# One FFN product moved to a later half, with three reorderings on VectorE around it

## The chip, the cores and the metric

The kernel runs on one core of a Trainium2 chip. The metric is the device time of one execution in microseconds, median over the runs.

## The reference

Cut to what is computed. The input has 64 sequences of 128 tokens with 256 channels, the context 128 tokens with 192 channels.

```python
def xattn(x, context, ...):                      # 16 heads of 64
    q_in = x @ Wq + lora(x, q_down, q_up)
    org, ipa = context[:, :-4], context[:, -4:]   # 124 and 4 tokens
    k_in = org @ Wk + lora(org, ...); v_in = org @ Wv + lora(org, ...)
    out = attention(q_in, k_in, v_in) + attention(q_in, ipa @ Wk_ipa, ipa @ Wv_ipa)
    return out @ Wo + bo + lora(out, o_down, o_up)

def ffn(x, w1, conv_w, conv_b, w2):
    h = bit_linear(x, w1)                         # x rounded to 8 bits per token, w to -1, 0, 1
    h = silu(depthwise_conv1d(h, conv_w, conv_b)) # 3 taps along the tokens, 1024 channels
    return bit_linear(h, w2)

x = x + xattn(layernorm(x), context, ...)
x = x + ffn(layernorm(x), w1, conv_w, conv_b, w2)
```

## The kernel before

The 64 sequences are taken in 16 groups of 4. Each engine runs its own program, written out by hand in one order, and they meet only at semaphores. One iteration of `run_groups` is one group's attention, in 32 **halves** (n = 0 to 31). Two halves are a **chunk**: one sequence and four heads. Iterations 0, 1, 15 and the two of the drain are written out, 2 to 14 are a loop.

In iteration g, `steps(g, n)` does four things side by side: the attention of group g, what is left of the projections of group g (`project(g, n + 32)`), the projections of group g + 1 (`project(g.shift(1), n)`), the FFN of group g - 1 (`finish(g.shift(-1), n)`) and the rest of the FFN of group g - 2 (`finish(g.shift(-2), n + 32)`). Tables at the head of the file say at which half a step stands: names in N_ for the projections, in M_ for the FFN. A place above 31 falls into the next iteration.

**PE** does, at each even half, `p_v` (L477, probabilities times V, three chunks back), `transpose_p` (L486, two chunks back), `scores` (L499, this chunk) and `project_out` (L512, four chunks back), and then what the tables put into the half: Q (L442), K (L451) and V (L461) products at N_Q, N_K, N_V plus N_QUAD, the transposes of the normalised x (L431) at N_XT = 8. For the FFN: the transposes of the quantised x2 at M_QT = 13 (L575), eight tiles of the first product into one PSUM bank, psF (L590, halves 15, 16, 17, 19, 20, 21, 23, 24), each waiting for the eviction of the one before, and the second product (L611), in two parts of two sequences, at M_F2 = (36, 38), so halves 4 and 6 of the iteration two after the group's own. The second part waits for the eviction of the first (`fin_done`).

**VectorE (DVE)**, at each even half, in `attend`: sums and reciprocals of the previous chunk (L903, L905), then the maxima of this chunk (L908, L909, L911), which wait for the scores. ACT's exponentials (L750) wait for these, and the next scores on PE wait for the exponentials. POOL (L1226) scales the probabilities by the reciprocals, and PE's transposes wait for it. Behind `attend` DVE does, in this order, the rest of its FFN steps of group g - 2, its projection steps and its FFN steps of group g - 1: the V copy (L896) from PSUM in halves 14, 22, 29 and 5, statistics of the next x, variance (L848, L851) at half 3, normalisation (L855) at half 6, the low parts of the context (L886, L887) at 8 and of x (L891) at 9, x2 = x + attention (L1029) at 4 and 7, normalisation, maximum and quantisation of x2 in halves 9 and 10 (L855, L1040, L1046, L1049). A tile of the first product is evicted to a GB buffer (L1063) in its own half. The convolution's middle tap is ACT's (L776), the other two are DVE's: `conv_before` (L998) one half later, `conv_next` (L992) two, and `gate` (L1004) three. The second product is evicted (L1020) two halves after it, M_FIN.

**POOL** raises the variance of the next x to the power -1/2 at half 4 (L1209), and adds the output bias to the residual (L1264). **SP** issues the DMAs in order: CRAW and RRAW at 7, the output at FINISH_HALVES - 1 (half 8), the K rows of the short context at 10, V rows at 10, 18, 26 and 1, XRES at 12.

HP holds the hidden layer, eight rows of 512 a partition. XN2 (the normalised x2) and Q1 (its quantised form) lie in its rows 6, 7 and 5, the quantised hidden layer Q2 in the first half of every row. GBS are the four GB buffers.

Of the kernel before, what the change touches and what calls it, by code (L numbers as in the profile page):

```python
# [51 lines left out]
U_Q, U_K, U_V = (0, 3), (1, 4), (2, 5)  # L52


N_STATS, N_VAR, N_POW, N_NORM = 0, 3, 4, 6
N_XT = 8
N_CIN = 7
N_CSPLIT = 8
# [13 lines left out]
M_F1 = 15  # L72
# [3 lines left out]
M_HMAX = M_F1 + M_TILE[-1] + M_HOFF  # L76
M_HT, M_BC2 = M_HMAX + 2, M_HMAX + 4
M_Q2 = M_HMAX + 5
M_F2 = (M_HMAX + 8, M_HMAX + 10)
M_COPY = M_Q2 + 2  # L80
L_X2, L_NORM, L_QT, L_F2 = (4, 5), 7, 13, M_HMAX + 8
Q2_PLACE = (0, 0, 1, 1)
# [64 lines left out]
def program(nc, x, ctxT, cipaT, Wq, Wk, Wv, Wo, bo, q_downT, q_up, k_downT, k_up, v_downT, v_up, o_downT, o_up,  # L147
            alphas, Wk_ipa, Wv_ipa, w1T, conv_w, conv_b, w2T, out):
    with ExitStack() as ctx:
# [63 lines left out]
        HT = [HP[:, j // 2, :, j % 2] for j in range(CT)]  # L213
        h_flat = HP[:].rearrange("p k t i -> p (k t i)")
        h_rows = h_flat.rearrange("p (j t) -> p j t", j=CT)
        XN2 = h_rows[:, 6:8, :].rearrange("p a (b d) -> p (a b) d", d=DM)
        Q1 = h_rows[:, 5, :].bitcast(BF16).rearrange("p (b d) -> p b d", d=DM)
        Q2 = [h_rows[:, j, 0:T // 2].bitcast(BF16) for j in range(CT)]
        OUTT = h_rows[:, 0:NB, T // 2:T]
        HM = GB[1]  # L220
# [619 lines left out]
        def _(dve):  # L840
# [30 lines left out]
            def project(g, n):  # L871
                if n in (N_STATS, N_STATS + 1):
                    if n == N_STATS:
                        dve.wait_ge(x_in, g.count(16, 16))
                    for b in range(2 * (n - N_STATS), 2 * (n - N_STATS) + 2):
                        m = dve.bn_stats(BS[0][:, b, :], XIN[:, b, :])
                    if n == N_STATS + 1:
                        m.then_inc(ln1_stats, 1)
                if n == N_VAR:
                    variance(g, 0, ln1_stats, ln1_mv, ln1_var)  # L880
                if n == N_NORM:
                    dve.wait_ge(ln1_rstd, g.count(1, 1))
                    normalise(0, XIN, XIN).then_inc(ln1_done, 1)
                if n == N_CSPLIT:
                    dve.wait_ge(c_high, g.count(1, 1))
                    dve.tensor_tensor(CTH[1][:], CRAW[:], CTH[0][:].bitcast(F32), ALU.subtract)  # L886
                    dve.tensor_tensor(CTR[64:128, :], RRAW[64:128, :], CTR[64:128, :].bitcast(F32), ALU.subtract).then_inc(c_split, 1)  # L887
                if n == N_XT + 1:
                    for k in range(2):
                        dve.wait_ge(xt_high, g.count(2, k + 1))  # L890
                        dve.tensor_tensor(XT[1][:, k, :], psU[k], XT[0][:, k, :].bitcast(F32), ALU.subtract).then_inc(unit_free[k], 1)  # L891
                q = quad_at(n - N_V[0] - 1)
                if q is not None:
                    u = 2 + 6 * q + U_V[0]
                    dve.wait_ge(unit_full, g.count(UNITS, u + 1))
                    dve.tensor_copy(V[0:ORG, 0:2, 256 * q:256 * q + 256],  # L896
                                    psU[u % 2][0:ORG, :].rearrange("p (b n) -> p b n", b=2)).then_inc(unit_free[u % 2], 1)

            def attend(g, s):
                gc, c = chunk_at(g, s - 1)  # L900
                if gc.exists():
                    dve.wait_ge(exp_done, gc.count(CHUNKS, c + 1))
                    dve.tensor_reduce(SU[c % 2][:, 4:8], SM[c % 2][:, :, ORG:TOK], AX.X, ALU.add).then_inc(sum_done, 1)  # L903
                    dve.wait_ge(sum_done, gc.count(CHUNKS, c + 1))
                    dve.reciprocal(RC[c % 2][:], SU[c % 2][:]).then_inc(rec_done, 1)  # L905
                if g.exists():
                    dve.wait_ge(s_full, g.count(CHUNKS, s + 1))
                    dve.tensor_reduce(MX[s % 2][:, 4:8], psS[:, :, ORG:TOK], AX.X, ALU.max, negate=True).then_inc(max_done, 1)  # L908
                    dve.tensor_reduce(MX[s % 2][:, 0:4], psS[:, :, 0:ORG], AX.X, ALU.max, negate=True)  # L909
                    dve.wait_ge(max_done, g.count(CHUNKS, s + 1))  # L910
                    dve.tensor_tensor(SM[s % 2][:, :, ORG:TOK], psS[:, :, ORG:TOK],  # L911
                                      MX[s % 2][:, 4:8].unsqueeze(2).broadcast_to([P, 4, IPA]), ALU.add).then_inc(sub_done, 1)
# [97 lines left out]
            def finish(g, n):  # L1010
# [30 lines left out]
                if n == M_NORM + M_SCALE:  # L1041
# [5 lines left out]
                    m.then_inc(q1_scaled, 1)  # L1047
                    dve.wait_ge(q1_scaled, g.count(1, 1))
                    dve.tensor_scalar(Q1, XN2, MAGIC, None, ALU.subtract).then_inc(q1_done, 1)  # L1049
                j = tile_at(n - M_F1 - M_LAG[2])  # L1050
                if 0 <= j < CT:
                    conv_next(g, j)
                j = tile_at(n - M_F1 - M_LAG[1])
                if 0 <= j < CT:
                    conv_before(g, j)
                j = tile_at(n - M_F1)
                if 0 <= j < CT:
                    dve.wait_ge(f1_full, g.count(CT, j + 1))
# [2 lines left out]
                    if j >= 4:  # L1061
                        dve.wait_ge(h_done, g.count(CT, j - 3))
                    dve.tensor_tensor(GB[j % 4].rearrange("p b t -> p (b t)"), psF, BC[:], ALU.mult).then_inc(g_done, 1)  # L1063
                j = tile_at(n - M_F1 - M_LAG[4])
                if 0 <= j < CT:
                    gate(g, j)
# [55 lines left out]
            low_part(2)  # L1122
            low_part(4)
            for n in range(EARLY_HALVES, HALVES):
                project(At(0), n)
                if n == LORA_O + 1:
                    dve.wait_ge(w_in[2], 16)
# [42 lines left out]

            def steps(g, n):
                if n % 2 == 0:
                    attend(g, n // 2)
                if g.reg is None and g.off == 0:
                    ternary(n)
                if g.shift(-2).exists():
# [135 lines left out]
```

## Time and profile before

| what | value |
|---|---|
| median of 3 runs | 1551.39 us (1551.12 to 1552.87) |
| the profiled execution | 1551.65 us |
| its span, first to last instruction | 1549.7 us |
| mean granted TensorE clock | 0.983 |
| PE busy | 1423.8 us, 92% |
| DVE busy | 1211.9 us, 78% |
| ACT busy | 1178.9 us, 76% |
| POOL busy | 661.4 us, 43% |
| POOL's power of the next x (L1209) | 1.02 us each |
| DMA, mean | 30 GB/s |

The page gives per engine the busy time and, for groups of instructions, the mean duration, the idle time just before them and what ended it. Matmul rows overlap, since their ends are modelled; what a step costs PE is read from start to start. The timeline gives the start, the duration, engine, line, operation, tiles (output <- inputs) and count of instructions in order of time, and in brackets the idle time before a row with its releaser.

### The profile page before, as it was taken

Reading aid. Unit: us, or ns where it says so; the run is one execution under the profiler, and the core shown is the slowest. Engines: PE = TensorE matmul, PEld = TensorE weight load, DVE = VectorE, ACT = ScalarE, POOL = GpSimd, SP = SyncE. Lnnn points to the kernel's source line nnn. Section 1 sums busy time; section 2 is a strip of 40 time slices with the busy share of each in tenths; the row PEclk is TensorE's granted clock in tenths of the full one; section 3 lists DMA queues with packets and bytes.
Section 4 is the critical chain, followed back from the end, with each engine's and each line's share of the span. In section 5 each row is a group of like instructions: output and inputs, shape, how many; then the busy total and the mean of one; then the engine's idle time right before and its main releaser. Section 6 shows DMA issues by size and latency. Waiting matters only on the chain.

```text
span 1549.7 us, 33116 instructions
## 1 busy us (share of the span) xinstructions
PE 1423.8 (92%) x10650; PEld 1157.1 (75%) x10650; DVE 1211.9 (78%) x3059; ACT 1178.9 (76%) x3909; POOL 661.4 (43%) x1058
## 2 busy tenths in 40 slices
PE   7899999999999999999999999999999999999772
PEld 4688788787877778787877878787787877878541
DVE  4363698887969888786988878798787878788788
ACT  3477787978878797887879787787978778796842
POOL 2354454444435444443544444444444444444520
PEclk9999999999999999999999999999999999999985
DMA  9100001000000100000010100001010000100000
GB/s 280 48 30 16 31 16 45 1 28 30 28 29 14 43 0 31 27 28 29 14 43 1 36 21 28 29 14 43 1 41 16 28 29 14 43 1 27 3 15 14
DMA packets 41144, 47.13 MB, mean 30 GB/s; under 512 B 3024, under 2 KB 35216, under 8 KB 41104
## 3 DMA queue, kind: packets, MB, share of 16 engines
q1 hardware_dynamic: 41104, 46.62, 9.7%
q8 instruction: 22, 0.36, 0.1%
q14 instruction: 18, 0.15, 0.0%
HBM read 36.13 MB, written 10.49 MB: 30 GB/s over the span
## 4 chain that ended last, share of the span: by engine, by line
PE 51%; DVE 20%; ACT 20%; issue 8%; DMA 1%; DVEq 0%; ACTq 0%; SPq 0%; POOL 0%
PE PS L499 10%; ACT SM L750 8%; PE PS L461 8%; PE PS L512 5%; PE PS L442 5%; PE PS L477 5%; PE PS L486 5%; PE PS L451 4%; PE PS L611 3%; ACT HP L776 2%; PE PS L590 2%; DVE GBS L1081 2%; DVE GBS L1063 2%; ACT QM L718 2%; ACT GBS L781 2%
## 5 line engine op out<-in xcount | busy, mean ns | idle before, releaser
L1226 POOL TENSOR_TENSOR SM<-SM,RC 128x496 f32<-128x496 f32 (+1 forms) x512 | 332.1, 670 | 743.5 <-DVE RC L905 743.5
L750 ACT ACTIVATE SM<-PS,MX 128x124 f32<-128x124 f32 x1024 | 359.4, 366 | 150.5 <-DVE SM L911 148.4
L499 PE MATMUL PS<-KT,QM 128*128 128x128 f32 x2048 | 277.8, 279 | 29.8 <-ACT SM L750 29.7
L499 PEld LDWEIGHTS PS<-KT,QM 128*128 128x128 f32 x2048 | 249.1, 192 | 45.4 <-ACT SM L750 44.7
L750 ACT ACTIVATION_READ_ACCUMULATOR SM<-PS,MX 128x1 f32 x1024 | 212.0, 207 | 0.0
L1257 POOL TENSOR_TENSOR OTl<-OF,OTh 128x256 fp32r<-128x256 f32 x256 | 198.5, 775 | 12.2 <-ACT OF L744 12.2
L742 ACT ACTIVATE OTh<-PS 128x256 fp32r<-128x256 f32 x256 | 100.4, 392 | 109.8 <-PE PS L477 108.7
L486 PE MATMUL PS<-IDF,SM 128*128 128x128 f32 x1024 | 168.4, 287 | 11.5 <-POOL SM L1226 11.3
L909 DVE TENSOR_REDUCE MX<-PS 128x4 f32<-128x496 f32 x256 | 170.0, 664 | 0.2 <-issue 0.2
L477 PE MATMUL PS<-PT,V 128*64 128x128 f32 x2048 | 168.8, 286 | 0.1
L477 PEld LDWEIGHTS PS<-PT,V 128*64 128x64 f32 x2048 | 106.9, 136 | 82.0 <-issue 74.8
L736 ACT ACTIVATE PT<-PS 128x512 f32<-128x512 f32 x256 | 156.9, 613 | 0.4 <-PE PS L486 0.4
L486 PEld LDWEIGHTS PS<-IDF,SM 128*128 128x128 f32 x1024 | 107.8, 141 | 57.8 <-issue 37.7
L908 DVE TENSOR_REDUCE MX<-PS 128x4 f32<-128x16 f32 x256 | 41.2, 161 | 124.9 <-PE PS L499 124.8
L776 ACT ACTIVATE HP<-GBS,CB,CW 128x512 f32<-128x512 f32 x128 | 111.3, 870 | 26.1 <-DVE GBS L1063 16.1
L1004 DVE SCALAR_TENSOR_TENSOR HP<-GBS,HP 128x512 f32<-128x512 f32 x128 | 109.1, 853 | 23.0 <-ACT GBS L781 22.2
L1063 DVE TENSOR_TENSOR GBS<-PS,BC 128x512 f32<-128x512 f32 x120 | 82.0, 683 | 54.7 <-PE PS L590 53.3
L512 PE MATMUL PS<-WOh,OTh 128*128 128x256 f32 x512 | 123.3, 322 | 0.7 <-POOL OTl L1257 0.7
L992 DVE SCALAR_TENSOR_TENSOR HP<-GBS,CW,HP 128x508 f32<-128x508 f32 x128 | 119.3, 932 | 0.1
L998 DVE SCALAR_TENSOR_TENSOR HP<-GBS,CW,HP 128x508 f32<-128x508 f32 x128 | 103.6, 809 | 17.6 <-ACT HP L776 14.1
L442 PE MATMUL PS<-XTh,WQh 128*128 128x512 f32 x256 | 107.2, 419 | 0.0
L512 PE MATMUL PS<-WOl,OTh 128*128 128x256 f32 x512 | 102.4, 281 | 0.0
(166 smaller groups left out, 3512.9 us busy)
## 6 DMA issues: line engine op xcount, KB each, us to landing
XIN<-in_x SPq DMA_DIRECT2D x16, 512.0 KB, 3.5
XRES<-in_x SPq DMA_DIRECT2D x16, 512.0 KB, 3.5
out_y<-HP SPq DMA_DIRECT2D x15, 512.0 KB, 3.0
CRAW<-in_ctxT SPq DMA_DIRECT2D x16, 256.0 KB, 2.7
RRAW<-in_ctxT SPq DMA_DIRECT2D x32, 128.0 KB, 2.8
QM<-in_Wq SPq DMA_DIRECT2D x1, 1024.0 KB, 9.0
GBS<-in_Wo SPq DMA_DIRECT2D x1, 1024.0 KB, 13.7
k_ipa_columns<-HP SPq DMA_DIRECT2D x1, 1024.0 KB, 5.1
```

Source lines behind the costliest of these rows:

```text
L442: m = mm(bank, WQ[w][:, k, P * tile:P * tile + P], XT[xt][:, k, :], start=(i == 0), stop=(i == 5))
L461: m = mm(bank[:, 256 * b:256 * b + 256], c[:, tok], w[:, cols], start=(i == 0), stop=(i == 4))
L477: m = mm(psO[r:r + DH, h // 2, :], V[:, b, DH * (4 * q + h):DH * (4 * q + h) + DH], PT[:, h, :], start=True, stop=True)
L486: m = pe.transpose(psT[:, h, :], SM[c % 2][:, h, :], IDF[:])
L499: m = mm(psS[:, h, :], QM[:, 2 * q + h // 2, h % 2, TOK * b:TOK * b + TOK], KT[:, 2 * q + h // 2, b, :], start=True, stop=True)
L512: m = mm(psY[b // 2][:, b % 2, :], OT[ot][c % 2][:, a, :], WO[w][:, 2 * q + a, :], start=(q == 0 and i == 0 and b % 2 == 0), stop=(q == QU ...
L736: act.activation(PT[:], psT, ACT.Identity).then_inc(pt_done, 1)
L750: m = act.activation(SM[s % 2][:, h, 0:ORG], psS[:, h, 0:ORG], ACT.Exp, bias=MX[s % 2][:, h:h + 1], accum_out=SU[s % 2][:, h:h + 1])
L776: act.activation(HT[j].rearrange("p (b t) -> p b t", b=NB), GB[j % 4], ACT.Identity, bias=CB[:, j:j + 1], scale=CW[:, j, 1:2]).then_inc(t1 ...
L909: dve.tensor_reduce(MX[s % 2][:, 0:4], psS[:, :, 0:ORG], AX.X, ALU.max, negate=True)
L1226: m = pool.tensor_tensor(part, part, RC[c % 2][:, 4 * i:4 * i + 4].unsqueeze(2).broadcast_to(shape), ALU.mult)
L1257: pool.tensor_tensor(OT[1][c % 2][:], OF[:], OT[0][c % 2][:].bitcast(F32), ALU.subtract).then_inc(ot_done, 1)
```

## The change

It does five things.

- M_F2 goes from (36, 38) to (36, 41): PE does the second FFN product of the second two sequences in half 9, not 6. Its eviction on DVE goes from half 8 to 11, and FINISH_HALVES with it, so SP's output DMA goes from half 8 to 11.
- XN2 and Q1 move out of HP into the GB buffers 2, 3 and 1.
- On DVE the eviction of a first-product tile stands ahead of the two taps of its half, not behind.
- On DVE the V copy stands between the sums and the maxima of a half. That changes the order in halves 14 and 22, where it stood behind the maxima; at 5 and 29 there are none.
- N_VAR, N_POW, N_NORM go from 3, 4, 6 to 5, 6, 7.

```diff
-N_STATS, N_VAR, N_POW, N_NORM = 0, 3, 4, 6
+N_STATS, N_VAR, N_POW, N_NORM = 0, 5, 6, 7
...
-M_F2 = (M_HMAX + 8, M_HMAX + 10)
+M_F2 = (M_HMAX + 8, M_HMAX + 13)
...
-        XN2 = h_rows[:, 6:8, :].rearrange("p a (b d) -> p (a b) d", d=DM)
-        Q1 = h_rows[:, 5, :].bitcast(BF16).rearrange("p (b d) -> p b d", d=DM)
+        gb_flat = GBS[:].rearrange("p i b t -> p (i b t)")
+        XN2 = gb_flat[:, 2 * T:4 * T].rearrange("p (b d) -> p b d", d=DM)
+        Q1 = gb_flat[:, T:2 * T].bitcast(BF16).rearrange("p (b d) -> p b d", d=DM)
...
-                j = tile_at(n - M_F1 - M_LAG[2])
-                if 0 <= j < CT:
-                    conv_next(g, j)
-                j = tile_at(n - M_F1 - M_LAG[1])
-                if 0 <= j < CT:
-                    conv_before(g, j)
                 j = tile_at(n - M_F1)
                 if 0 <= j < CT:
                     dve.wait_ge(f1_full, g.count(CT, j + 1))
...
+                j = tile_at(n - M_F1 - M_LAG[2])
+                if 0 <= j < CT:
+                    conv_next(g, j)
+                j = tile_at(n - M_F1 - M_LAG[1])
+                if 0 <= j < CT:
+                    conv_before(g, j)
...
             def steps(g, n):
                 if n % 2 == 0:
-                    attend(g, n // 2)
+                    attend_sums(g, n // 2)
+                if g.exists():
+                    value_copy(g, n + HALVES)
+                if g.shift(1).exists(1):
+                    value_copy(g.shift(1), n)
+                if n % 2 == 0:
+                    attend_maxima(g, n // 2)
```

The rows below are from the loop's iteration. In them `x16` and `x2` are counts, `REGISTER_ALU` is the arithmetic of a wait, and the lines of the changed file are one to five higher.

On PE in halves 6 to 9, from half 6's output product; before:

```order
L512 MATMUL PS<-WOh,OTl 128x256 x2
L131 REGISTER_ALU
L451 MATMUL PS<-CTh,WKh 128x512
L451 MATMUL PS<-CTl,WKh 128x512
L451 MATMUL PS<-CTh,WKl 128x512
L451 MATMUL PS<-CTR,WKRh 128x512
L451 MATMUL PS<-CTR,WKRl 128x512
L607 REGISTER_ALU
L611 MATMUL PS<-W,HP 128x256 x16
L461 MATMUL PS<-WVh,CTh 128x256
```

And now, from half 8's output product:

```order
L513 MATMUL PS<-WOh,OTl 128x256 x2
L428 REGISTER_ALU
L131 REGISTER_ALU
L432 MATMUL PS<-IDF,XIN 128x128 x8
L608 REGISTER_ALU
L612 MATMUL PS<-W,HP 128x256 x16
L478 MATMUL PS<-PT,V 64x128 x4
L487 MATMUL PS<-IDF,SM 128x128 x4
```

The 16 matmuls of the second product stood between K and V and now stand behind the transposes of x, ahead of half 10's chunk.

On DVE from half 8 to the start of half 10, before:

```order
L911 TENSOR_TENSOR SM<-PS,MX 128x4x4
L1020 SCALAR_TENSOR_TENSOR HP<-PS,AD,HP 128x256 x2
L886 TENSOR_TENSOR CTl<-CRAW,CTh 128x512
L887 TENSOR_TENSOR CTR<-RRAW,CTR 64x512
L890 REGISTER_ALU
L891 TENSOR_TENSOR XTl<-PS,XTh 128x512
L890 REGISTER_ALU
L891 TENSOR_TENSOR XTl<-PS,XTh 128x512
L855 TENSOR_SCALAR HP<-X,MV,RS 128x256 x4
L1040 TENSOR_REDUCE AR<-HP 128x4
L903 TENSOR_REDUCE SU<-SM 128x4
```

And where the eviction stands now, at the end of half 10's steps and in half 11:

```order
L1051 TENSOR_SCALAR GBS<-GBS,AS 128x256 x4
L1054 TENSOR_SCALAR GBS<-GBS 128x1024
L1025 SCALAR_TENSOR_TENSOR HP<-PS,AD,HP 128x256 x2
L906 TENSOR_REDUCE SU<-SM 128x4
L908 RECIPROCAL RC<-SU 128x8
```

The eviction of the second product left its place ahead of the low parts and stands ahead of the sums of half 12.

On DVE in halves 20 to 22, from the maxima of half 20; before:

```order
L998 SCALAR_TENSOR_TENSOR HP<-GBS,CW,HP 128x4x127
L1058 REGISTER_ALU
L1063 TENSOR_TENSOR GBS<-PS,BC 128x512
L1004 SCALAR_TENSOR_TENSOR HP<-GBS,HP 128x512
L992 SCALAR_TENSOR_TENSOR HP<-GBS,CW,HP 128x4x127
L998 SCALAR_TENSOR_TENSOR HP<-GBS,CW,HP 128x4x127
L1058 REGISTER_ALU
L1063 TENSOR_TENSOR GBS<-PS,BC 128x512
L903 TENSOR_REDUCE SU<-SM 128x4
L905 RECIPROCAL RC<-SU 128x8
L907 REGISTER_ALU
L908 TENSOR_REDUCE MX<-PS 128x4
```

And now:

```order
L1057 REGISTER_ALU
L1062 TENSOR_TENSOR GBS<-PS,BC 128x512
L1003 SCALAR_TENSOR_TENSOR HP<-GBS,CW,HP 128x4x127
L1009 SCALAR_TENSOR_TENSOR HP<-GBS,HP 128x512
L1057 REGISTER_ALU
L1062 TENSOR_TENSOR GBS<-PS,BC 128x512
L997 SCALAR_TENSOR_TENSOR HP<-GBS,CW,HP 128x4x127
L1003 SCALAR_TENSOR_TENSOR HP<-GBS,CW,HP 128x4x127
L906 TENSOR_REDUCE SU<-SM 128x4
L908 RECIPROCAL RC<-SU 128x8
L898 REGISTER_ALU
L899 COPY V<-PS 124x2x256
```

Each eviction (L1062) stands ahead of its half's taps, and the V copy, which followed the maxima of half 22, stands ahead of them.

## Rows read from the trace of the kernel before

**Rows 1.** One loop period: us; PE, PEld, DVE, ACT, POOL busy; PEclk; DMA

```profile
701.80:791.95 90.15, 85.96 (x662) 70.67 (x661) 74.19 (x190) 72.47 (x244) 40.22 (x66) 1.00 0.08 25
```

**Rows 2.** Who PE waited for, whole run (us in total, times, longest)

```profile
PE PS L499 <- ACT SM L750: 29.7, 62, 1.1
...
PE PS L590 <- DVE GBS L1063: 17.8, 31, 2.5
```

**Rows 3.** Timeline of PE, halves 6 to 14 (start, us, line, tiles, count, idle)

```profile
701.80 1.92 PE L611 MATMUL PS<-W,HP 128*128 128x256 bf16 x16
703.47 0.36 PE L461 MATMUL PS<-WVh,CTh 128*128 128x256 f32 x1
...
704.82 0.66 PE L477 MATMUL PS<-PT,V 128*64 128x128 f32 x8
...
707.50 1.04 PE L431 MATMUL PS<-IDF,XIN 128*128 128x128 f32 x8
...
709.06 0.66 PE L486 MATMUL PS<-IDF,SM 128*128 128x128 f32 x4
710.66 1.16 PE L499 MATMUL PS<-KT,QM 128*128 128x128 f32 x8 [0.95 <-ACT SM L750]
...
715.67 0.66 PE L486 MATMUL PS<-IDF,SM 128*128 128x128 f32 x4
716.66 1.16 PE L499 MATMUL PS<-KT,QM 128*128 128x128 f32 x8 [0.34 <-ACT SM L750]
...
720.68 0.66 PE L486 MATMUL PS<-IDF,SM 128*128 128x128 f32 x4
721.17 1.06 PE L499 MATMUL PS<-KT,QM 128*128 128x128 f32 x8
```

**Rows 4.** Timeline of ACT, halves 8 to 12

```profile
708.14 1.09 ACT L711 ACTIVATE XTh<-PS 128x512 fp32r<-128x512 f32 x2
709.11 0.37 ACT L750 ACTIVATE SM<-PS,MX 128x124 f32<-128x124 f32 x1
...
715.12 0.36 ACT L750 ACTIVATE SM<-PS,MX 128x124 f32<-128x124 f32 x1 [3.37 <-DVE SM L911]
...
719.33 0.37 ACT L750 ACTIVATE SM<-PS,MX 128x124 f32<-128x124 f32 x1
```

**Rows 5.** Timeline of DVE, halves 8 to 12

```profile
707.00 0.17 DVE L908 TENSOR_REDUCE MX<-PS 128x4 f32<-128x16 f32 x1 [1.01 <-PE PS L499]
...
707.75 0.86 DVE L1020 SCALAR_TENSOR_TENSOR HP<-PS,AD,HP 128x256 f32<-128x256 f32 x2
708.53 0.94 DVE L886 TENSOR_TENSOR CTl<-CRAW,CTh 128x512 fp32r<-128x512 f32 x1
...
714.27 0.16 DVE L908 TENSOR_REDUCE MX<-PS 128x4 f32<-128x16 f32 x1
...
718.16 0.16 DVE L903 TENSOR_REDUCE SU<-SM 128x4 f32<-128x16 f32 x1
```

**Rows 6.** Timeline of DVE, halves 21 and 22

```profile
744.21 1.21 DVE L992 SCALAR_TENSOR_TENSOR HP<-GBS,CW,HP 128x508 f32<-128x508 f32 x1
745.34 0.73 DVE L998 SCALAR_TENSOR_TENSOR HP<-GBS,CW,HP 128x508 f32<-128x508 f32 x1
...
747.64 0.68 DVE L896 COPY V<-PS 124x512 f32<-124x512 f32 x1
```

**Rows 7.** Timeline of POOL, half 20

```profile
743.70 1.18 POOL L1264 TENSOR_TENSOR XRES<-XRES,BO 128x256 f32<-128x256 f32 x1
```

**Rows 8.** Timeline of PE, halves 23 and 28

```profile
748.37 0.51 PE L451 MATMUL PS<-CTh,WKh 128*128 128x512 f32 x1 [0.37 <-DVE V L896]
...
761.37 1.16 PE L499 MATMUL PS<-KT,QM 128*128 128x128 f32 x8 [0.21 <-ACT SM L750]
```

**Rows 9.** Timeline of ACT, half 22

```profile
746.71 0.85 ACT L776 ACTIVATE HP<-GBS,CB,CW 128x512 f32<-128x512 f32 x1 [1.08 <-DVE GBS L1063]
...
748.00 0.35 ACT L750 ACTIVATE SM<-PS,MX 128x124 f32<-128x124 f32 x1
```

More of the change, by code:

```diff
@@ L891, in project, with value_copy @@
                         dve.tensor_tensor(XT[1][:, k, :], psU[k], XT[0][:, k, :].bitcast(F32), ALU.subtract).then_inc(unit_free[k], 1)
+            def value_copy(g, n):
                 q = quad_at(n - N_V[0] - 1)
@@ L897, in project, with attend_sums @@
                                     psU[u % 2][0:ORG, :].rearrange("p (b n) -> p b n", b=2)).then_inc(unit_free[u % 2], 1)
-            def attend(g, s):
+            def attend_sums(g, s):
                 gc, c = chunk_at(g, s - 1)
@@ L905, in attend, with attend_maxima @@
                     dve.reciprocal(RC[c % 2][:], SU[c % 2][:]).then_inc(rec_done, 1)
+            def attend_maxima(g, s):
                 if g.exists():
@@ L1124, in _ @@
             for n in range(EARLY_HALVES, HALVES):
+                value_copy(At(0), n)
                 project(At(0), n)
```

## The prediction

> **What bounds the kernel now.** I compared the engines over one period, then read the totals of the waits, and then followed single chunks of that period in the timelines of PE, DVE and ACT. One group's pass through the loop is 90.15 us (701.80 to 791.95); PE is busy for 85.96 of it, DVE for 74.19, ACT for 72.47 and POOL for 40.22, at a granted clock of 1.00, the 2.4 GHz level [rows 1]. So PE is the bound, and a gain can only come from the moments in which it stands. Over the run the largest of these in the loop are the score products waiting for ACT's exponentials (29.7 us) and the first FFN product waiting for DVE's eviction (17.8 us) [rows 2].
>
> Where they lie shows in the starts of consecutive rows. The transposes before a score product need 0.49 us when nothing is waited for (720.68 to 721.17). In half 10 the same step takes from 709.06 to 710.66, 1.60 us, so PE stands 1.11; in half 12 from 715.67 to 716.66, 0.99, so it stands 0.50 [rows 3]. Both are one loop: scores, maxima on DVE, exponentials on ACT, next scores. In half 8 PE has only a chunk's own products and the eight transposes of x: the chunk ends 3.65 us after it began (704.82 to 708.47). The chunk before it holds K, V and the second FFN product. The work is there, but in the wrong chunk.
>
> **The product moved.** It costs PE 1.67 us (701.80 to 703.47) [rows 3], the same in either place. Taken out of half 6, it lets PE reach half 8 at 703.15 instead of 704.82, and I replay from there:
> - The transposes of x start at 707.50 - 1.67 = 705.83, and ACT's copy of them at 706.47 instead of 708.14. ACT does the exponentials of half 8 behind that copy, at 707.44 instead of 709.11 [rows 3, 4]. The maxima that these need stood 1.01 us waiting for PE [rows 5]; with PE early DVE starts them at 705.99 and they are through by 706.8, so they don't stand in the way.
> - Scores follow the start of the exponentials by 1.55 us (709.11 to 710.66), so those of half 10 may start at 708.99. PE, with the product behind the transposes of x (706.80 to 708.47), gets there at 709.65. It no longer waits. That is 1.01 us earlier than 710.66.
> - Scores of half 10 to the next chunk is 4.37 us (710.66 to 715.03), so PE is ready for the scores of half 12 at 715.15.
>
> **The evictions of the product moved from half 8 to half 11.** It is 0.86 us in the row and 0.79 to the next start [rows 5]. In half 8 it stood ahead of the low parts of the context and of x. DVE is rid of it there and of the wait of 1.01, and so is 1.8 us earlier at the maxima of half 10. Those low parts now fall on POOL's scaling of the probabilities, and a DVE operation with two SBUF inputs that meets POOL is longer: 1.21 us beside POOL's 1.18, against 0.73 for its neighbour over as many elements [rows 6, 7]. The bounds are 0 and 0.48 for one meeting; the low part of the context already shows 0.94 us, and I take 0.2. So the maxima come at 714.27 - 1.8 + 0.2 = 712.67, the exponentials at 713.52, the scores may start at 715.06, and PE, ready at 715.15, doesn't wait: 1.51 earlier than 716.66.
>
> The Trainium skill says of this (SBUF — State Buffer, section "Who interferes with whom") that a DVE instruction with two SBUF inputs contends with a GpSimd one that reads SBUF, and that the later to start blocks until the other is through. By that rule the low part would wait out POOL's instruction rather than share, an estimate of 0.4 to 0.7 us in place of my 0.2, the gain at half 14 below would be 0.6 to 0.9, and the time 1541 to 1545. The stretched row [rows 6] agrees with the rule.
>
> In half 11 the eviction comes back, between the quantisation and the sums of half 12. From the maxima of half 10 to those sums is 3.89 us (714.27 to 718.16); with 0.79 more they start at 712.67 + 4.68 = 717.35, the exponentials 1.17 later (718.16 to 719.33) at 718.52, and the scores of half 14 may start at 720.07 [rows 4, 5]. PE, 3.43 us from scores to the next chunk, would be ready at 719.66. So a new stall of 0.41 us stands in half 14, and the scores start at 720.07 instead of 721.17 [rows 3]. **Gain up to here: 1.10 us a group** of the 1.61 that PE stood.
>
> **V copies ahead of maxima.** The one at half 14 falls into DVE's wait for the scores: nothing. The one at half 22 is different. There the maxima did not wait for PE, so the copy (0.60 us to the next start) goes straight onto the path to the exponentials of half 22, which start at 748.00. It buys the K product of half 23 its 0.37 us stall [rows 6, 8], but from 748 to 761 ACT has no gap, and the scores of half 28 wait for it at 761.37 [rows 8, 9]. What PE gains in between, it gives back there; what ACT loses, PE loses.
>
> **Evictions ahead of taps.** The first two F1 products stand in adjacent halves with only V between, so the eviction cannot come before the product and stays the bound: no gain. At halves 19 and 20 DVE comes to the eviction 0.3 to 0.5 us before PE has the product, and now stands with the taps queued behind; but the taps then leave POOL's busy stretch, and 0.48 us of stretching goes with that. At half 21 the eviction starts near 744.3, not 746.0, and ACT's wait of 1.08 us for it goes [rows 9]. That leaves DVE at the sums of half 22 between 0.4 us earlier and 0.3 later. With the V copy the exponentials of half 22 are 0 to 0.6 us late (bounds: a full 0.6 from the copy and 0.3 from the taps, less ACT's own lead of 1.08, to nothing). I take **0.15 us lost** a group, since the eviction's lead nearly pays the copy.
>
> **Variance two halves later, and the buffers.** Variance, power and normalisation of the next x stay ahead of what needs them: DVE still normalises between the eviction of half 6 and x + attention, the same row order. Half 3 loses 0.5 us of DVE work, beside PE's first FFN product: nothing. POOL's power leaves half 4 for half 6, with several us before the transposes that follow: nothing. If that cover went, the power's 1.0 us would stand before a transposition. The normalised x2 and its quantised form in the GB buffers cost the same instructions. The output DMA goes out on SP behind the loads of half 10, about 9 us after its old place, and XRES behind it; ACT needs its landing only in half 16: nothing.
>
> **The sum.** 1.10 - 0.15 = 0.95 us for each of the 13 groups of the steady loop that hold the product, 12.4 us, and 0.6 for the last iteration, which has no projections and where DVE leads (estimate: the same 1.4 from moving the product, less 0.79 for the eviction put back). In the drain the rows stand in the same order: 0. Together 13.0. The profiled execution took 1551.65 (span 1549.7 and 1.95 around it), near the median of 1551.39; 1551.4 - 13.0 = **1538.4**.
>
> **The rivals.**
> - *More comes through* (chance 0.12): ACT's gapless stretch starts earlier, since the eviction in half 21 leads, and the K stall (0.37), the F1 stall before it (some 0.2) and the 0.41 of half 14 are kept as well. 1.10 + 0.57 = 1.7, and 2.0 with a part of the last: 13 x 1.7 + 0.6 and 13 x 2.0 + 0.6, 1529 to 1525. Against it: the V copy on the way to the exponentials.
> - *No change* (0.10): what is gained by half 14 is given back where the scores wait for ACT in half 28, with the exponentials of half 22 late by 0.6 and the meetings with POOL at 0.48: 1.10 - 0.28 - 0.6 = 0.2 a group, 1548.8. For it: that ACT stretch. Against: what starts it is itself a group's work after half 16, and moves earlier with PE.
> - *Slower* (0.07): at halves 16, 19 and 20 DVE stands at evictions for products not yet there, and the three taps behind each meet POOL. 3 x 0.48 = 1.4, and 0.6 for the copy, is 2.0 on the path to the exponentials of half 22. It decides once that passes 1.10: 13 x 0.9 = 12 us slower, 1563. Against: DVE stands while POOL works, so the taps should miss it.
> - *My forecast* (0.71): 0.4 to 1.3 a group, 1534 to 1546.
>
> Range **1529 to 1549**: below it lies most of the first rival, above it the slower one and a part of no change. A measurement of this kernel tells about 0.2%, 3.1 us, from no change. Faster 0.83 (forecast and first rival), same 0.10, slower 0.07.
>
> **What would show it.** Right: the period is 89.0 to 89.5; the scores of half 10 and 12 follow their transposes by 0.5; in half 14 a new short wait for ACT appears; K in half 23 no longer waits for the V copy; scores of half 28 still wait for ACT. Wrong: a wait of over 0.5 us in half 12 (the low parts met POOL), or over 1.2 in half 28 (taps or V copy late), or a wait of the Q1 transposes in half 13 for the eviction now in half 11.

## The result, and the profile after

| kernel | median | lowest to highest | runs |
|---|---|---|---|
| before | 1551.9 us | 1551.12 to 1552.87 | 4 |
| changed | 1535.58 us | 1534.94 to 1538.8 | 4 |

The ratio is 0.9898, with a 95% interval of 0.9885 to 0.991: faster by 16 us, 1.0%. The forecast was 1538.4 in a range of 1529 to 1549. The profiled execution has a span of 1533.5 us (before 1549.7), at the same mean granted clock, 0.983.

[Rows 1] runs from one second product to the next. That product now stands in another half, so periods are counted from the scores of half 6 to the next; the kernel before has 90.15 that way too. One period of the changed kernel (us, then the busy time of PE, PEld, DVE, ACT and POOL, clock, DMA):

```profile
692.99:782.01 89.02, 85.11 (x659) 70.90 (x661) 72.86 (x189) 72.77 (x245) 40.81 (x66) 1.00 0.08 25
```

89.02 where before it was 90.15: 1.13 us a group. Over the loop its periods lie between 89.00 and 89.10. Who PE waited for over the run, the rows that answer to [rows 2]:

```profile
PE PS L500 <- ACT SM L751: 24.0, 48, 1.1
...
PE PS L487 <- POOL SM L1238: 16.5, 35, 1.7
PE PS L591 <- DVE GBS L1062: 14.1, 16, 2.3
```

The middle row was 11.3 us in 19 waits before. What is new is a wait of 0.30 to 0.38 in half 28 of every group, ahead of scores that wait for ACT there anyway.

The timeline of PE in halves 8 to 14, the rows that answer to [rows 3] (start, us, line, tiles, count, idle):

```profile
700.58 1.91 PE L612 MATMUL PS<-W,HP 128*128 128x256 bf16 x16
...
703.01 0.66 PE L487 MATMUL PS<-IDF,SM 128*128 128x128 f32 x4
703.50 1.06 PE L500 MATMUL PS<-KT,QM 128*128 128x128 f32 x8
...
708.35 0.66 PE L487 MATMUL PS<-IDF,SM 128*128 128x128 f32 x4
708.95 1.16 PE L500 MATMUL PS<-KT,QM 128*128 128x128 f32 x8
...
712.96 0.66 PE L487 MATMUL PS<-IDF,SM 128*128 128x128 f32 x4
713.87 1.16 PE L500 MATMUL PS<-KT,QM 128*128 128x128 f32 x8 [0.26 <-ACT SM L751]
```

The step from the transposes to the scores is 0.49 in half 10 (it was 1.60), 0.60 in half 12 (0.99) and 0.91 in half 14 (0.49). So the stalls of 1.11 and 0.50 are gone but for 0.11, and a new one of 0.42 stands in half 14. Counted from the scores of half 6 of its own period, each kernel reaches the scores at (us, start of scores):

| half | before | changed | earlier by |
|---|---|---|---|
| 10 | 11.64 | 10.51 | 1.13 |
| 12 | 17.64 | 15.96 | 1.68 |
| 14 | 22.15 | 20.88 | 1.27 |
| 16 | 29.08 | 27.92 | 1.16 |
| 22 | 45.81 | 44.32 | 1.49 |
| 24 | 52.25 | 50.11 | 2.14 |
| 28 | 62.35 | 61.20 | 1.15 |
| next 6 | 90.15 | 89.02 | 1.13 |

What half 16 has is all that is left at the end. The extra of halves 22 to 26 (the K product no longer waits for the V copy, the first-product tiles no longer for their evictions) is given back in half 28, where PE now waits 0.82 us for ACT and not 0.21 [rows 8].

### The profile page after: what moved, and what is told of

Read it like the earlier page. It is cut to its first block, busy times and chain, and to the rows that moved or that the text cites. A ratio compares the mean times of both kernels' runs of the same rounds, so it can differ in the third digit from the quotient of the medians.

```text
span 1533.5 us, 33070 instructions
## 1 busy us (share of the span) xinstructions
PE 1409.5 (92%) x10604; PEld 1159.5 (76%) x10650; DVE 1195.5 (78%) x3059; ACT 1182.3 (77%) x3909; POOL 668.1 (44%) x1058
## 4 chain that ended last, share of the span: by engine, by line
PE 43%; DVE 30%; ACT 17%; issue 9%; DMA 1%; DVEq 0%; POOL 0%; SPq 0%; POOLq 0%; ACTq 0%
PE PS L500 10%; ACT SM L751 8%; PE PS L462 6%; PE PS L443 5%; PE PS L513 5%; PE PS L478 4%; PE PS L487 4%; PE PS L452 3%; PE PS L591 2%; DVE HP L1003 2%; DVE GBS L1062 2%; DVE MX L914 2%; DVE GBS L1086 2%; DVE HP L1009 2%; ACT QM L719 2%
## 5 line engine op out<-in xcount | busy, mean ns | idle before, releaser
L1238 POOL TENSOR_TENSOR SM<-SM,RC 128x496 f32<-128x496 f32 (+1 forms) x512 | 324.2, 654 | 738.6 <-DVE RC L908 738.6
L1269 POOL TENSOR_TENSOR OTl<-OF,OTh 128x256 fp32r<-128x256 f32 x256 | 204.1, 797 | 10.4 <-ACT OF L745 10.4
L1062 DVE TENSOR_TENSOR GBS<-PS,BC 128x512 f32<-128x512 f32 x120 | 82.5, 688 | 89.6 <-PE PS L591 88.6
L997 DVE SCALAR_TENSOR_TENSOR HP<-GBS,CW,HP 128x508 f32<-128x508 f32 x128 | 110.0, 860 | 0.1
L1003 DVE SCALAR_TENSOR_TENSOR HP<-GBS,CW,HP 128x508 f32<-128x508 f32 x128 | 97.3, 760 | 11.8 <-ACT HP L777 11.8
L745 ACT ACTIVATE OF<-PS 128x256 f32<-128x256 f32 x256 | 100.8, 394 | 5.4 <-POOL OTl L1269 5.4
```

The source lines that it names most:

```text
L1003: dve.scalar_tensor_tensor(out=y[:, :, 1:TOK], in0=GB[j % 4][:, :, 0:TOK - 1], scalar=CW[:, j, 0:1], in1=y[:, :, 1:TOK], op0=ALU.mult, op1 ...
L1238: m = pool.tensor_tensor(part, part, RC[c % 2][:, 4 * i:4 * i + 4].unsqueeze(2).broadcast_to(shape), ALU.mult)
L1269: pool.tensor_tensor(OT[1][c % 2][:], OF[:], OT[0][c % 2][:].bitcast(F32), ALU.subtract).then_inc(ot_done, 1)
```

## Experiments

Each kernel is the changed one with the edit shown, or the one before where that is said. Times are medians, and periods are read as above. The kernel before took 1552.1, 1553.02 and 1551.02 us beside the three sets in which these ran.

**1. The product alone: the kernel before with the new M_F2 and the new places of XN2 and Q1** (the changed file's lines for these, not repeated here).

```diff
-M_F2 = (M_HMAX + 8, M_HMAX + 10)
+M_F2 = (M_HMAX + 8, M_HMAX + 13)
```

> The kernel before with only the product moved to half 9 (its eviction to half 11, XN2 and Q1 in the GB buffers). Evictions behind taps, V copies behind maxima, variance at half 3 as before. Theory P (the product is the gain): the scores of half 10 follow their transposes by 0.5 us, the period falls from 90.15 to 88.9-89.2, and the time is 1534 to 1538. Rival O (the orders on VectorE bring half or more of it): the gain of half 14 is lost again by half 28, period 89.6 or more, 1543 or more.

Measured: 1535.57 us (1535.21 to 1536.76, 4 runs), ratio 0.9896 (0.988 to 0.9913), period 89.04. That is the changed kernel's time.

**2. The orders alone: the changed kernel with M_F2 as before.**

```diff
-M_F2 = (M_HMAX + 8, M_HMAX + 13)
+M_F2 = (M_HMAX + 8, M_HMAX + 10)
```

> The changed kernel with the product put back to half 6 (eviction in half 8). Evictions ahead of taps, V copies ahead of maxima, variance at half 5 stay. Theory P: the waits of 1.1 us in half 10 and 0.5 in half 12 are back, period 90.0 to 90.3, 1549 to 1553. Rival O: period 89.6 or less, 1544 or less.

Measured: 1551.74 us (1550.39 to 1553.58, 10 runs), ratio 0.9998 (0.9988 to 1.0008), period 90.16. PE's timeline in halves 10 and 12 has the two old stalls again, to a hundredth:

```profile
708.55 0.66 PE L487 MATMUL PS<-IDF,SM 128*128 128x128 f32 x4
710.16 1.16 PE L500 MATMUL PS<-KT,QM 128*128 128x128 f32 x8 [0.95 <-ACT SM L751]
...
715.17 0.66 PE L487 MATMUL PS<-IDF,SM 128*128 128x128 f32 x4
716.16 1.16 PE L500 MATMUL PS<-KT,QM 128*128 128x128 f32 x8 [0.33 <-ACT SM L751]
```

The gain is the product's, and the three other edits together are worth nothing. That left open whether each is worth nothing, or two cancel.

**3. The V copy of half 22 behind the maxima again.**

```diff
-                if g.shift(1).exists(1):
+                if g.shift(1).exists(1) and n != 22:
                     value_copy(g.shift(1), n)
                 if n % 2 == 0:
                     attend_maxima(g, n // 2)
+                if g.shift(1).exists(1) and n == 22:
+                    value_copy(g.shift(1), n)
```

> The changed kernel with the V copy of half 22 behind the maxima again; that of half 14 stays ahead. Theory: in half 22 DVE is on the path to ACT's gapless stretch (ACT stands 1.11 us before the exponentials of half 22), so the copy's 0.58 us comes off the period, 88.4 to 88.6, and the time is 1527 to 1529; the K product of half 23 waits 0.3 to 0.5 us for the copy, which costs nothing. Rival (the copy releases PE): period 89.0 to 89.3, 1535 to 1539.

Measured: 1528.87 us (1528.17 to 1530.35, 4 runs), ratio 0.9849 (0.9833 to 0.9866), period 88.46. It beats both kernels.

**4. Taps ahead of evictions again, V copies ahead of the maxima as changed.** The two tap blocks of the diff move back ahead of the eviction.

> The changed kernel with the two taps ahead of the eviction again; the product in half 9 and the V copies ahead of the maxima stay. Theory: on VectorE the new order of the evictions is worth about the 0.56 us a group that the V copy of half 22 costs, and the two only cancelled (period 89.02 with both, 89.03 with neither, 88.46 with the evictions alone). Then the period is 89.5 to 89.7 and the time 1542 to 1544. Rival: where the V copy stands ahead, the order of taps and evictions makes no difference, since ACT's gapless stretch behind half 22 starts at the same time: period 89.0, 1535 to 1537.

Measured: 1541.04 us (1540.29 to 1542.49, 4 runs), ratio 0.9929 (0.9912 to 0.9946), period 89.34. That lies between the theory and the rival: the order matters with the V copy ahead too, but by less than I expected.

**5. Both V copies behind the maxima.** As experiment 3, for half 14 too.

> The changed kernel with both V copies, of halves 14 and 22, behind the maxima; the product in half 9 and the evictions ahead of the taps stay. Theory: in half 14 the V copy falls into VectorE's wait for the scores, so that its place is worth nothing there: period 88.4 to 88.5, 1528 to 1530, as with the copy of half 22 alone. Rival: behind the maxima of half 14 it comes too late for the K product of half 15, which waits 0.3 to 0.5 us: period 88.8 to 89.0, 1532 to 1536.

Measured: 1528.9 us (1528.21 to 1529.47, 4 runs), ratio 0.9846 (0.983 to 0.9863), period 88.47: the place in half 14 is worth nothing.

Experiments 1, 3, 4 and 5 make a square (period, median):

| | taps first | evictions first |
|---|---|---|
| V copy of half 22 behind the maxima | 89.04, 1535.57 | 88.46, 1528.87 and 1528.90 |
| V copy of half 22 ahead of them | 89.34, 1541.04 | 89.02, 1535.58 (changed) |

Both edits have a price, but what it is depends on the other edit. The order of the evictions gains 0.58 us a group with the V copy behind the maxima (6.7 us in the medians) and 0.32 with it ahead (5.5 us). The V copy costs 0.30 with the taps first (5.5 us) and 0.56 with the evictions first (6.7 us). From the corner with neither to the one with both, they cancel. (The medians also hold what is outside the loop, where the four kernels differ too: from the transposes of the quantised x2 in iteration 15 to the end it is 113.6 us with neither, 115.2 with the evictions first, 113.7 with the V copy ahead and 113.1 with both.) The start of the exponentials of half 22, counted from the scores of half 6, moves as the period does: 47.84 with neither, 47.23 with the evictions first, 48.16 with the V copy ahead, 47.82 with both. Where neither is in (experiment 1), ACT is late from its wait for the eviction of half 21 and comes to the exponentials 0.29 us after the maxima are ready (740.03), so about half of the copy is hidden when it is added there (DVE, then ACT):

```profile
739.86 0.17 DVE L912 TENSOR_TENSOR SM<-PS,MX 128x16 f32<-128x16 f32 x1
```

```profile
740.32 0.35 ACT L751 ACTIVATE SM<-PS,MX 128x124 f32<-128x124 f32 x1
```

With the evictions first ACT stands ready and all of the copy counts. ACT in halves 21 and 22 of the changed kernel, and DVE beside it:

```profile
738.24 0.92 ACT L777 ACTIVATE HP<-GBS,CB,CW 128x512 f32<-128x512 f32 x1
738.98 0.72 ACT L782 ACTIVATE GBS<-HP 128x512 f32<-128x512 f32 x1
740.81 0.36 ACT L751 ACTIVATE SM<-PS,MX 128x124 f32<-128x124 f32 x1 [1.11 <-DVE SM L916]
```

```profile
737.13 0.68 DVE L1062 TENSOR_TENSOR GBS<-PS,BC 128x512 f32<-128x512 f32 x1
737.73 0.73 DVE L997 SCALAR_TENSOR_TENSOR HP<-GBS,CW,HP 128x508 f32<-128x508 f32 x1
738.39 0.74 DVE L1003 SCALAR_TENSOR_TENSOR HP<-GBS,CW,HP 128x508 f32<-128x508 f32 x1
...
739.37 0.67 DVE L899 COPY V<-PS 124x512 f32<-124x512 f32 x1
739.95 0.16 DVE L913 TENSOR_REDUCE MX<-PS 128x4 f32<-128x16 f32 x1
```

With the V copy behind the maxima (experiment 3, ACT and then PE):

```profile
737.41 0.36 ACT L751 ACTIVATE SM<-PS,MX 128x124 f32<-128x124 f32 x1 [0.51 <-DVE SM L916]
```

```profile
738.02 0.50 PE L452 MATMUL PS<-CTh,WKh 128*128 128x512 f32 x1 [0.35 <-DVE V L899]
...
750.85 1.16 PE L500 MATMUL PS<-KT,QM 128*128 128x128 f32 x8
```

With taps first (experiment 4), ACT:

```profile
741.27 0.85 ACT L777 ACTIVATE HP<-GBS,CB,CW 128x512 f32<-128x512 f32 x1 [1.09 <-DVE GBS L1068]
742.02 0.64 ACT L782 ACTIVATE GBS<-HP 128x512 f32<-128x512 f32 x1
742.91 0.37 ACT L751 ACTIVATE SM<-PS,MX 128x124 f32<-128x124 f32 x1 [0.25 <-DVE SM L916]
```

ACT stands 1.1 us or more in half 21 or 22 in each of these forms: for the eviction ([rows 9], and 1.09 here, with 0.25 more for the maxima), or, once the eviction leads, for the maxima of half 22 (1.11). Only with the V copy out of the way does the wait fall, to 0.51. And what the exponentials of half 22 do, the scores of half 28 repeat:

```profile
754.19 1.16 PE L500 MATMUL PS<-KT,QM 128*128 128x128 f32 x8 [0.82 <-ACT SM L751]
```

From the first to the second it is 13.37 us before (748.00 to 761.37), 13.38 in the changed kernel (740.81 to 754.19) and 13.44 in experiment 3 (737.41 to 750.85). The K stall of 0.35 that the V copy was moved for comes back there and costs nothing, since PE otherwise waits later.

**6. The eviction of half 11 cut to 8 of 256 columns.** It leaves out most of the FFN's share for half of the output, so its time says only what the eviction costs where it stands.

```diff
+                            w = DM if c == 0 else 8
...
-                            m = dve.scalar_tensor_tensor(out=OUTT[:, b, :], ...
+                            m = dve.scalar_tensor_tensor(out=OUTT[:, b, 0:w], ...
```

> The changed kernel, but the eviction in half 11 takes 8 of 256 columns a sequence, so half of the output lacks most of the FFN: it measures what the eviction costs in its new place. Theory: the wait of 0.42 us in half 14 goes and the period is 88.5 to 88.7. Rival (the wait in half 14 comes from ACT's or POOL's place in the order, not from the eviction): the wait stays at 0.3 or more and the period at 88.9 to 89.1.

Measured: 1528.12 us (one run), period 88.48. DVE around the eviction, and PE at the scores of half 14:

```profile
708.05 0.35 DVE L1026 SCALAR_TENSOR_TENSOR HP<-PS,AD,HP 128x8 f32<-128x8 f32 x2
708.32 0.16 DVE L906 TENSOR_REDUCE SU<-SM 128x4 f32<-128x16 f32 x1
```

```profile
710.64 0.66 PE L487 MATMUL PS<-IDF,SM 128*128 128x128 f32 x4
711.13 1.06 PE L500 MATMUL PS<-KT,QM 128*128 128x128 f32 x8
```

The sums of half 12 follow 0.27 us behind the start of the eviction instead of 0.78 (710.38 to 711.16 in the changed kernel), the scores follow their transposes by 0.49 again, and the group is 0.54 us shorter.

**7. The eviction in half 12, behind the maxima, where DVE stands for ACT.** Nothing is left out.

```diff
-M_FIN = 2
+M_FIN = (2, 3)
```

> The changed kernel with the eviction of the second product of the second two sequences in half 12, behind the maxima, where VectorE then stands 1.7 us for ACT, and not in half 11 ahead of the sums; the output DMA follows it to half 12. Nothing is left out. Theory: in half 11 the eviction costs what the kernel gained when it was cut to 8 columns, 0.54 us a group, and in half 12 it is free: the stall of half 14 goes from 0.42 to under 0.1, period 88.4 to 88.6, 1527 to 1530. Rival: PE comes to the transposes of the quantised x2 in half 13 before the eviction frees their bank, or the output DMA holds up the residual's load, and what is gained is given back: a wait of 0.3 to 0.9 there, period 88.9 to 89.2, 1534 to 1538.

Measured: 1536.78 us (1536.32 to 1537.35, 4 runs), ratio 0.99 (0.9883 to 0.9916), period 89.04. The theory falls and the rival holds. The stall of half 14 is gone, but PE waits for the same eviction before the transposes of the quantised x2, whose bank it frees (DVE, then PE):

```profile
711.26 0.87 DVE L1025 SCALAR_TENSOR_TENSOR HP<-PS,AD,HP 128x256 f32<-128x256 f32 x2
```

```profile
712.28 0.61 PE L576 MATMUL PS<-IDB,GBS 128*128 128x128 bf16 x8 [0.46 <-DVE HP L1025]
```

I had looked for a gap on DVE and not at how near the next user of the bank is: the transposes would have started at about 711.7, and the eviction, even behind the maxima, ends at 712.1.

**8. Experiments 3 and 7 together.**

> The changed kernel with the V copy of half 22 behind the maxima and the eviction of the second product in half 12 behind the maxima. Nothing is left out. Theory: the two costs lie in different halves (14 and 22) of one chain and add: 0.56 + 0.54 us a group, period 87.9 to 88.1, 1520 to 1523. Rival: they are the same slack counted twice; the earlier start of the exponentials is then lost to PE, which becomes the bound from half 14 to 28: period 88.3 to 88.5, 1526 to 1529.

Measured: 1531.05 us (1529.18 to 1531.43, 4 runs), period 88.53: experiment 3 and 0.07 us a group more. With the later eviction the scores of half 16 stand 27.99 us behind those of half 6, here and in experiment 7, where it is 27.92 without it. The time agrees with neither expectation, since the later eviction gains nothing by itself.

**9. Experiments 5 and 6 together** (it leaves out the same share of the FFN as 6).

> The changed kernel with both V copies behind the maxima and the eviction in half 11 cut to 8 of 256 columns; it leaves out most of the FFN's share for half of the output. Theory: the 0.54 us of the eviction (half 14) and the 0.56 us of the V copy (half 22) are two delays of one chain and add: period 87.9 to 88.1, 1520 to 1523. Rival: whichever goes first leaves little for the other, because PE is then the bound from half 14 to 28: period 88.3 to 88.5, 1526 to 1529.

Measured: 1521.21 us (1520.99 to 1521.44, 4 runs), ratio 0.9805 (0.9788 to 0.9821), period 87.93. The gains of 0.54 and 0.56 add to within a hundredth (89.02 - 87.93 = 1.09): two delays of one chain, in different halves, and not one slack counted twice.

**10. The low parts of the context cut to 8 of 512 columns, from the second group on.** It leaves out most of that correction of the K and V products.

```diff
+                    w = 512 if g.reg is None and g.off == 0 else 8
...
-                    dve.tensor_tensor(CTH[1][:], CRAW[:], CTH[0][:].bitcast(F32), ALU.subtract)
+                    dve.tensor_tensor(CTH[1][:, 0:w], CRAW[:, 0:w], CTH[0][:, 0:w].bitcast(F32), ALU.subtract)
```

> The changed kernel whose two low parts of the context take 8 of 512 columns, from the second group on; it leaves out most of that correction of the K and V products. Theory: the longer rows of POOL in half 8 (1.64 us for the scaling, 1.53 for the power) come from VectorE's low parts beside them: they go back to 1.19 and 1.01, and ACT's wait of 0.39 for POOL with them. Scores of half 10 and 12 don't move by more than the 0.1 us that PE still stood in half 12, but VectorE, 1.3 us earlier, takes away the stall of 0.42 in half 14: period 88.5. Rival: POOL's rows stay at 1.64 and 1.53, and something else in that half stretches them.

In the changed kernel the low part on DVE and POOL's scaling and power (of x2's variance) lie side by side in half 8 (DVE, then POOL):

```profile
700.60 0.99 DVE L887 TENSOR_TENSOR CTl<-CRAW,CTh 128x512 fp32r<-128x512 f32 x1
701.61 0.69 DVE L888 TENSOR_TENSOR CTR<-RRAW,CTR 64x512 fp32r<-64x512 f32 x1
```

```profile
700.03 1.64 POOL L1238 TENSOR_TENSOR SM<-SM,RC 128x496 f32<-128x496 f32 x2 [5.96 <-DVE RC L908]
701.63 1.53 POOL L1244 TENSOR_TENSOR RS<-VE,HALF 128x4 f32<-128x4 f32 x1
```

The first of POOL's rows is two instructions. Shown one by one:

```profile
700.03 1.01 POOL L1238 TENSOR_TENSOR SM<-SM,RC 128x496 f32<-128x496 f32 x1 [5.96 <-DVE RC L908]
701.01 0.66 POOL L1238 TENSOR_TENSOR SM<-SM,RC 128x16 f32<-128x16 f32 x1
```

Measured with the low parts cut: 1525.3 us (one run), period 88.26. POOL's two rows, then the two scaling instructions one by one, then DVE:

```profile
696.16 1.19 POOL L1239 TENSOR_TENSOR SM<-SM,RC 128x496 f32<-128x496 f32 x2 [5.96 <-DVE RC L909]
697.30 1.01 POOL L1245 TENSOR_TENSOR RS<-VE,HALF 128x4 f32<-128x4 f32 x1
```

```profile
696.16 1.01 POOL L1239 TENSOR_TENSOR SM<-SM,RC 128x496 f32<-128x496 f32 x1 [5.96 <-DVE RC L909]
697.13 0.21 POOL L1239 TENSOR_TENSOR SM<-SM,RC 128x16 f32<-128x16 f32 x1
```

```profile
696.73 0.47 DVE L888 TENSOR_TENSOR CTl<-CRAW,CTh 128x8 fp32r<-128x8 f32 x1
697.21 0.17 DVE L889 TENSOR_TENSOR CTR<-RRAW,CTR 64x8 fp32r<-64x8 f32 x1
```

So the meeting takes place, and on POOL it costs 0.45 + 0.52 us; ACT's wait for POOL, 0.39 in the changed kernel, is gone too. The single instructions show what happens: the engines take turns, and only the later one pays.

- The large scaling instruction (128x496) starts first and takes 1.01 us with the subtraction beside it and with it cut.
- The subtraction starts 0.57 us into it and takes 0.30 more than alone (0.69, see below). Cut to 8 columns, it takes 0.47 where its neighbour of 8 columns takes 0.17: again 0.30 more, for a sixty-fourth of the elements. That is a wait and not a slower rate.
- The small scaling instruction (128x16) comes while the subtraction runs and takes 0.66 and not 0.21.
- The power starts 0.02 us behind the second low part and takes 1.53 and not 1.01, while that low part has its 0.69 as in the first group, where POOL is idle.

Take from each late instruction the time that it needs alone, and its wait ends 0.13 to 0.15 us before the recorded end of the one ahead of it, in all four.

The period is 0.24 shorter than I expected: scores of half 12 come 0.10 earlier and those of half 14 0.62, and by half 16 it is 0.73. The first FFN product of half 15 waits for ACT's broadcast of the scales in both kernels, and that starts 0.72 us earlier (24.93 us behind the scores of half 6, and 25.65 in the changed kernel). The cut takes 1.05 us from DVE (the low part of x starts 8.29 us behind the scores of half 6, and 9.34 in the changed kernel; I had expected 1.3) and the waits from POOL together, so this run doesn't say what POOL's waits alone cost the group.

**11. Variance, power and normalisation of the next x back in halves 3, 4 and 6.**

```diff
-N_STATS, N_VAR, N_POW, N_NORM = 0, 5, 6, 7
+N_STATS, N_VAR, N_POW, N_NORM = 0, 3, 4, 6
```

> The changed kernel with variance, power and normalisation of the next x back in halves 3, 4 and 6; all else as changed. Theory: these steps lie off the path in either place: period 89.0, 1534.5 to 1536.5. Rival: in half 8 the power stands behind POOL's scaling and both are stretched by the low parts of the context (0.45 and 0.52 us more than before); with the power gone from there, ACT's wait for POOL in half 8 goes and a little reaches PE: period 88.8 or less, 1532 or less. On the other side, 0.5 us of VectorE work back in half 3 could delay half 4, where PE stands: 1539 or more.

Measured: 1535.58 us (1535.38 to 1537.99, 4 runs), ratio 0.9902 (0.9885 to 0.9918), period 88.98: nothing, to the hundredth the changed kernel's median. The rival was also wrong in its premise: POOL's rows of half 8 read 1.64 and 1.53 here too, since the power there is x2's and not that of the next x.

## Why the prediction was right, point by point

**The product moved** was right in mechanism and size. By half 10 I had 1.01 us and it is 1.13, by half 12 1.51 and 1.68. 0.10 us of it is a slip: the second product ends at 708.47 in my replay, and 0.59 and 0.49 us for the chunk's two steps [rows 3] give 709.55, not 709.65. Experiment 1 shows that this step alone makes the whole difference, and experiment 2 that nothing else does.

**The meeting with POOL** was the term of 0.2, and it was mis-sized. The low part went from 0.94 us to 0.99, so the term is 0.05. Most of the meeting was in the row of before already: in the first group, with no row of POOL beside it, the same instruction takes 0.69 (the row below, of the changed kernel), and before the change it met POOL's low part of the attention's output instead (708.19 to 708.93). I had noted the 0.94 and still added 0.2 to it. The maxima of half 10 start 13.48 us behind the scores of half 6, and 13.65 was forecast (712.67 less 699.02).

```profile
18.80 0.69 DVE L887 TENSOR_TENSOR CTl<-CRAW,CTh 128x512 fp32r<-128x512 f32 x1 [9.80 <-ACT CTR L708]
```

The rule of the Trainium skill (SBUF — State Buffer, "Who interferes with whom") that I weighed says that the later to start blocks until the other is through. The trace agrees: the low part paid 0.30 us beside a scaling instruction that kept its 1.01, and POOL's two later instructions paid 0.45 and 0.52 (experiment 10). My estimate of 1541 to 1545 for that rule didn't come, but for other reasons: 0.25 of the 0.30 already stood in the row before, and the transposes of half 10, which need POOL's scaling, don't wait for it. So the rule was right and my price for it was wrong, and a meeting has a price on POOL that I had left out.

**The eviction put back in half 11** was right: a stall of 0.41 was forecast in half 14 and 0.42 stands there. Experiment 6 shows its cause; what is left of it without the eviction is nothing. The gain in half 14 is 1.27, where 1.10 was forecast, and most of the difference is the 0.15 of the meeting. But I stopped there and took it for the gain of the group. By half 16 it is 1.16: the first FFN product of half 15 waits for ACT's broadcast of the scales in both kernels, and that comes only 1.16 us earlier (26.81 and 25.65 us behind the scores of half 6; before, then changed):

```profile
725.83 0.60 ACT L770 ACTIVATE BC<-PS 128x512 f32<-128x512 f32 x1
```

```profile
718.64 0.60 ACT L771 ACTIVATE BC<-PS 128x512 f32<-128x512 f32 x1
```

That my 1.10 lies so near the 1.13 of the period is in part luck: a term 0.15 too large and a loss of 0.11 that I hadn't looked for.

**V copies and evictions** were forecast to lose 0.15 together and lose nothing (period 89.04 in experiment 1, which has neither, and 89.02 with both). The sign of each was right, "the eviction's lead nearly pays the copy", and so was where it shows. Two steps in the working failed. "Evictions ahead of taps: no gain" at halves 16 and 17 was right (the scores of halves 16, 18 and 20 stand within 0.01 us of experiment 1), but at halves 20 to 22 the order is worth 0.58 with the V copy behind the maxima, and 0.32 with it ahead. My bounds on DVE's arrival at the sums of half 22 ran from 0.4 earlier to 0.3 later, and it is 0.36 earlier: the taps did leave POOL's busy stretch (0.73 and 0.74 us at 737.73 and 738.39, where the first in [rows 6] has 1.21). And ACT's wait of 1.08 "goes" only as a wait for the eviction; it comes back as 1.11 for the maxima. With the evictions first the V copy costs 0.56, near the upper bound that I named. Both numbers were in the text, but only their sum was worked out, not the kernel that has the one without the other. That the sum is nil and not a loss is no finding on either edit.

**Variance, buffers and DMAs** were right: nothing (experiments 11 and 1). XRES now lands later, and POOL waits for it by 0.3 us in the period shown, off the path.

**The sum.** 13 groups at 1.13 are 14.7 us where I had 12.4. From the first transposes of the quantised x2, in iteration 1, to those of iteration 14 the change is 14.93 us. The last iteration was forecast at 0.6. It loses 0.23 up to those transposes (85.39 us after those before, where it was 85.16) and gains 0.58 from there to its last scores, so 0.35. The loss is what I had named as the sign of being wrong, a wait of these transposes for the eviction of half 11. It stands there once, in the iteration without projections:

```profile
1418.80 0.48 PE L513 MATMUL PS<-WOh,OTh 128*128 128x256 f32 x2
...
1420.44 0.61 PE L576 MATMUL PS<-IDB,GBS 128*128 128x128 bf16 x8 [0.69 <-DVE HP L1025]
```

A further 0.79 us was there before any second product: the first transposes of x start at 89.86 instead of 90.65. I had nothing for this and don't put it down to the change. In the profiles of the study that start lies between 89.64 and 90.89, whichever edits are in, and the first 90 us are loads and set-up. Together 0.79 + 14.93 + 0.35 = 16.07 of the 16.2 by which the spans differ; the rest lies behind the last scores.

The forecast of the time was 2.8 us high (1538.4 against 1535.58). Against the profiled spans it was 3.2 (13.0 of 16.2): 2.5 in the steady loop, of which a third is the 0.06 a group by half 16 and the rest the 0.12 behind it, 0.79 of the start and some 0.1 behind the last scores, less 0.25 in the last iteration.

**The rivals.** More comes through (1529 to 1525) didn't happen in this kernel, but experiment 3 is in it: 1528.87, once the V copy is off the way to the exponentials, which was the reason against it. No change and slower failed with their common premise that the meetings with POOL or the taps reach the exponentials; the eviction in front of the taps avoids them instead.

## What to carry to other kernels

Move work out of the chunk in which the bound engine arrives late at a hand-over and into one where it arrives early, and then look at the hand-over after next: here 1.50 of 1.61 us of stalls went, and 0.42 came back in half 14, from an eviction of 0.8 us put back on the other engine. When several orders change together, cross them: two edits that cancel look like two that do nothing, and undoing the bad one was worth 6.7 us. Run all four corners, since each edit's worth can depend on the other (0.58 or 0.32 us a group for the one, 0.56 or 0.30 for the other). Before a wait is removed, follow it to the next place where the same engine waits; if it stands there anyway, the wait was free, and what one puts ahead of the other engine's work to remove it is not. And a free gap on one engine is only a place for a step if the next user of what it frees comes later still. A row of several merged instructions can hide which of them paid: look at them one by one before you say that two engines share.

## What the runs showed of the hardware

- Where a DVE subtraction with two SBUF inputs met POOL's instructions, the later to start waited and the earlier lost nothing. The subtraction of 128x512 takes 0.69 us alone and 0.99 behind POOL's scaling, which keeps its 1.01; the 128x16 and the power that come behind the two subtractions go from 0.21 to 0.66 and from 1.01 to 1.53, and both are back at 0.21 and 1.01 when the subtractions are cut (experiment 10). POOL's loss, 0.97 us over two instructions, is three times DVE's, 0.30.
- The wait doesn't depend on how much the waiting instruction has to do: 0.30 us for 512 columns and for 8, both started 0.57 us into the scaling, and 0.52 for a power on 128x4 elements. It ends 0.13 to 0.15 us before the recorded end of the instruction ahead, in the four cases looked at.
- Cut from 256 to 8 columns each, the two evictions go from 0.87 us to 0.35, and what follows starts 0.27 us behind the first instead of 0.78: a third of the time is left for 3% of the columns.
